# A relational graph sum on one core: its last 1024 nodes as dense products instead of gathered edge tiles

## The chip, the cores and the metric

The kernel runs on one core of a Trainium2 chip. The core has five engines that run side by side, each through its own list of instructions: PE (matrix products), DVE (vector), ACT (scalar functions), POOL (general, and the one that issues the gathers) and SP (which issues plain DMAs). They meet at semaphores only. The metric is the device time of one execution in microseconds (us), lower is better.

## The reference

There are N = 3125 nodes with D = 128 features and E = 103125 edges, sorted by destination. 3125 of them are loops; on average 33 edges end at a node.

```
# first part: 3 graph convolutions, a linear layer on all 4 states
h = elu(segment_sum((h @ W.T)[src] * dinv[src] * dinv[dst], dst) + b) + h     # 3 times
x = layernorm(x + concat(h0, h1, h2, h3) @ lin_w.T + lin_b)
# second part, the "second sum": 8 relations from 4 bases
W[r] = sum over b of w_comp[r, b] * bases[b]
msg  = x[src] * edge_weight
agg[r, n] = sum of msg over the edges of type r that end at n
x = layernorm(x + sum over r of agg[r] @ W[r])
```

All four bases can be summed first: for each node n and base b, A[b, n] = sum over its edges of (edge_weight * w_comp[type, b]) * x[src], and the result is the sum over b of A[b, n] @ bases[b]. Both kernels compute it so.

## The kernel before, in words

**Layers.** The 3 convolutions go as dense products: the adjacency is built on the chip as counts (one-hots by DVE at L865, products on PE at L1134, copied to bytes by ACT at L719, in blocks of 20 nodes), and PE multiplies with it in 7 column chunks of 480 nodes a layer (L1145). PE is busy nearly all of this time. Small DVE work between the chunks (the line numbers round L904, L923) computes `coef`, the edge's weight times the 4 base coefficients, for all 806 tiles. The linear layer (L1232) and the first layernorm follow; its result x1 is stored to memory by SP (L584).

**Second sum.** The edges are cut into 806 tiles of 128 (one edge per partition). 33 tiles make a chunk, meant for 128 destination nodes, and there are 25 chunks (the last has 14 tiles). Each tile takes three steps:

- POOL gathers the tile's 128 source rows of x1 from memory with one indirect DMA (`gathers`, L661), 11 tiles to a group. Ahead of a group it waits until DVE has written the group's indices (`indices`, L1002) and until PE is done with the group's old rows (a wait on `s_mu`, tile done, L654), and runs a tiny operation (L659).
- DVE makes a 128x192 matrix (`moving`, L1012): for each edge a one-hot of its destination in a window of 48 nodes, times its 4 coefficients. There are MS = 3 buffers, so DVE waits before tile j until PE has signalled that tile j - 3 is done.
- PE multiplies the gathered rows with it (`tile`, L1252), adding into PSUM banks 2, 0, 1 (nodes before, in and after the chunk); 12 of 33 tiles straddle two banks and need two products. A product of fp32 numbers appears as two passes in the trace. Every tile raises `s_mu`.

Once per chunk come the `fold` on DVE (L1020, L1021: banks 0 and 1 to SBUF), three products with zeros on PE that clear the banks (L1265), the sum `aggf` (L1050), 4 products with the bases (`finish`, L1258), and the layernorm (L1028 to L1038, root on ACT at L778), stored by SP. The previous chunk's closing work lies between the tiles of the next one. The engines' programs are written out by hand in this order, as loops over chunks.

Of the kernel before, what the change touches and what calls it, by code (L numbers as in the profile page):

```python
# [16 lines left out]
def build_program(nc, x, src, dst, etype, eweight, conv_w, conv_b, lin_w, lin_b, bases, w_comp, out):  # L17
# [18 lines left out]
    NCHK = -(-TILES // TPB)  # L36
    LTILES = TILES - TPB * (NCHK - 1)
    LNODES = N - P * (NCHK - 1)
# [33 lines left out]
    with ctx:  # L72
# [6 lines left out]

        arena = sb("arena", [P, ADJ], bf16)  # L80
# [60 lines left out]
        flagf = carve(47904, 4, fp32, 4)  # L141
        excess = sb("excess", [P, 1], fp32)
# [11 lines left out]
        srcI = carve(14592, TILES, u32, 4)  # L154
        dl = carve(17920, TILES, fp32, 4)
        wE = carve(RB + 12544, TILES, fp32, 4)
        tyE = carve(RB + 15872, TILES, fp32, 4)
        linbB = carve(RB + 19200, D, fp32, 4)
        coef = carve(2 * RB + 12800, TILES * NB, fp32, 4).rearrange("p (t b) -> p t b", b=NB)
        relw = carve(2 * RB + 25696, TILES, fp32, 4)  # L160
        xb = carve(4 * RB, NBLK * D, fp32, 4).rearrange("p (s d) -> p s d", s=NBLK)
        acc = carve(4 * RB + 12800, NB * P, fp32, 4)
        carry = carve(4 * RB + 14848, NB * P, fp32, 4)
        aggf = carve(4 * RB + 16896, NB * P, fp32, 4).rearrange("p (b n) -> p b n", b=NB)
        bnst = carve(4 * RB + 18944, UBT * 8, fp32, 4).rearrange("p (t s) -> p t s", t=UBT)
        mv = carve(4 * RB + 19072, NBLK * 2, fp32, 4).rearrange("p (t s) -> p t s", s=2)
        rstd = carve(4 * RB + 19328, NBLK, fp32, 4)
        iota_w = carve(4 * RB + 19456, WN, fp32, 4)
        shift = carve(4 * RB + 20224, NBLK, fp32, 4)
        iota_wf = carve(4 * RB + 19712, P, fp32, 4)  # L170
        ystage = carve(4 * RB + 20480, 2 * D, fp32, 4).rearrange("p (s d) -> p s d", s=2)
        fst = carve(4 * RB + 21504, 16, fp32, 4)
        idxg = carve(4 * RB + 21632, TPB, u32, 4)
        x1r = carve(2 * RB, NCHK * D, fp32, 4).rearrange("p (s d) -> p s d", s=NCHK)
# [33 lines left out]
        x1_d = nc.dram_tensor("x1_scratch", [N, D], fp32, kind="Internal").ap()  # L208

        ps = ctx.enter_context(nc.psum_tensor("ps", [P, 8, 512], fp32))  # L210


        s_dst = sem("dst_loaded")
        s_raw = [sem(f"edges_loaded{a}") for a in range(4)]
# [1088 lines left out]
```

## Time and profile before

| | |
|---|---|
| 3 runs | 1859.42, 1865.01 (median), 1873.81 us |
| profiled execution | 1863.87 us, of which its span is 1862.1 us (1.8 us lie around it) |
| busy share of the span | PE 62%, DVE 43%, POOL 44%, ACT 14% |
| busy time | PE 1147.9 us, DVE 792.9, POOL 820.8, ACT 257.6 |
| granted TensorE clock, mean | 0.698 of full |
| first gather of the second sum to the end | from 563.5 to 1862.1 us |

The profile page is one execution. It gives busy time by engine, the span in 40 slices, the groups of instructions that cost most with the idle time before them and what ended it, and the chain that ended last. The timeline rows give the start of an operation, its length, and in brackets how long its engine had been idle and whose signal ended that: "issue" is no signal at all that the profile shows, "remote" one that it cannot assign.

### The profile page before, as it was taken

Reading aid. Unit: us, or ns where it says so; the run is one execution under the profiler, and the core shown is the slowest. Engines: PE = TensorE matmul, PEld = TensorE weight load, DVE = VectorE, ACT = ScalarE, POOL = GpSimd, SP = SyncE. Lnnn points to the kernel's source line nnn. Section 1 sums busy time; section 2 is a strip of 40 time slices with the busy share of each in tenths; the row PEclk is TensorE's granted clock in tenths of the full one; section 3 lists DMA queues with packets and bytes.
Section 4 is the critical chain, followed back from the end, with each engine's and each line's share of the span. In section 5 each row is a group of like instructions: output and inputs, shape, how many; then the busy total and the mean of one; then the engine's idle time right before and its main releaser. Section 6 shows DMA issues by size and latency. Waiting matters only on the chain.

```text
span 1862.1 us, 18954 instructions
## 1 busy us (share of the span) xinstructions
PE 1147.9 (62%) x6042; PEld 841.1 (45%) x6042; DVE 792.9 (43%) x1636; ACT 257.6 (14%) x630; POOL 820.8 (44%) x931
## 2 busy tenths in 40 slices
PE   2478999999982455555554555565545455555446
PEld 2455666455471344344443434444434333444445
DVE  3798996455661333233332232333323323333324
ACT  3498894002030000000000000000000000000000
POOL 4220000000006666665555656655556556556562
PEclk8679999999995656556655655656565656656666
DMA  4500001001112111111111111111111111111110
GB/s 126 178 15 2 1 1 35 1 1 35 35 27 88 43 45 42 47 45 41 41 39 41 42 41 45 48 39 41 38 41 45 39 44 47 41 41 44 39 44 24
DMA packets 51315, 77.86 MB, mean 42 GB/s; under 512 B 18282, under 2 KB 35159, under 8 KB 50628
## 3 DMA queue, kind: packets, MB, share of 16 engines
q0 software_dynamic: 26512, 54.60, 10.6%
q1 hardware_dynamic: 24756, 22.61, 4.1%
q8 instruction: 32, 0.52, 0.1%
q14 instruction: 15, 0.12, 0.0%
HBM read 65.48 MB, written 6.88 MB: 39 GB/s over the span
## 4 chain that ended last, share of the span: by engine, by line
PE 43%; another core or an unknown queue 19%; DVE 16%; issue 14%; DVEq 3%; DMA 2%; POOL 1%; ACT 1%; SPq 0%; ACTq 0%; POOLq 0%
PE ps L1252 24%; PE ps L1145 13%; DVE arena L1012 6%; DVE arena L865 4%; DVEq L1012 2%; PE ps L1265 2%; PE ps L1258 2%; PE ps L1134 1%; PE ps L1232 1%; DVE arena L1021 1%; DVE arena L1020 1%; PE ps L1161 1%; DVE arena L847 1%; POOL arena L627 1%
## 5 line engine op out<-in xcount | busy, mean ns | idle before, releaser
L1252 PE MATMUL ps<-arena 128*128 128x192 f32 (+9 forms) x2200 | 616.9, 440 | 562.2 <-DVE arena L1012 413.0
L661 POOL DMA_INDIRECT arena<-x_scratch,arena x806 | 761.6, 945 | 241.0 <-issue 233.7
L1252 PEld LDWEIGHTS ps<-arena 128*128 128x128 f32 x2200 | 489.3, 291 | 694.2 <-DVE arena L1012 500.2
L1012 DVE SCALAR_TENSOR_TENSOR arena<-ps,arena 128x192 f32<-128x192 f32 x806 | 323.6, 416 | 877.4 <-remote 389.2
L1145 PE MATMUL ps<-arena,u 125*128 125x480 fp8e5 (+1 forms) x1575 | 359.7, 353 | 0.5 <-ACT arena L721 0.5
L1145 PEld LDWEIGHTS ps<-arena,u 125*128 125x128 bf16 x1575 | 151.0, 97 | 103.8 <-ACT arena L721 1.0
L865 DVE TENSOR_TENSOR arena<-arena 128x2048 bf16<-128x2048 bf16 (+2 forms) x158 | 188.7, 1254 | 11.0 <-PE ps L1134 7.2
L778 ACT ACTIVATE arena<-arena,epst 128x1 f32<-128x1 f32 x25 | 7.4, 294 | 1293.4 <-issue 891.9
L642 POOL IOTA arena<- 128x48 f32 x1 | 0.2, 176 | 396.0 <-PE ps L1145 396.0
L1134 PE MATMUL ps<-arena 128*128 128x125 bf16 x1256 | 149.0, 233 | 33.8 <-DVE arena L865 31.8
L1134 PEld LDWEIGHTS ps<-arena 128*128 128x128 bf16 x1256 | 107.0, 104 | 85.4 <-DVE arena L865 49.6
L659 POOL TENSOR_TENSOR arena<-epst 128x1 f32<-128x1 f32 x74 | 14.5, 195 | 293.4 <-issue 178.5
L721 ACT ACTIVATE arena<-ps,minus 128x500 bf16<-128x500 f32 x157 | 109.7, 699 | 0.0
L719 ACT CAST arena<-ps 128x500 fp8e5<-128x500 f32 x157 | 91.4, 582 | 37.2 <-PE ps L1134 36.0
L1265 PE MATMUL ps<-arena 128*128 128x512 bf16 x75 | 36.5, 625 | 57.7 <-DVE arena L1021 51.3
L904 DVE TENSOR_TENSOR work<-ps,dinv_all 128x480 f32<-128x480 f32 (+1 forms) x21 | 13.0, 621 | 101.7 <-PE ps L1145 101.7
L923 DVE SCALAR_TENSOR_TENSOR arena<-arena,compB 128x806 f32<-128x806 f32 x28 | 47.0, 1680 | 1.0
L1258 PEld LDWEIGHTS ps<-arena 128*128 128x128 f32 x200 | 45.9, 318 | 2.3 <-DVE arena L1065 2.3
L1258 PE MATMUL ps<-arena 128*128 128x128 f32 x200 | 45.3, 403 | 2.0 <-DVE arena L1065 2.0
L736 ACT ACTIVATE work<-work 128x480 f32<-128x480 f32 (+1 forms) x21 | 12.2, 579 | 197.4 <-DVE work L906 197.4
L1265 PEld LDWEIGHTS ps<-arena 128*128 128x128 bf16 x75 | 7.0, 123 | 70.3 <-DVE arena L1021 56.8
L721 ACT ACTIVATION_READ_ACCUMULATOR arena<-ps,minus 128x1 f32 x157 | 34.4, 219 | 0.0
(124 smaller groups left out, 507.2 us busy)
## 6 DMA issues: line engine op xcount, KB each, us to landing
arena<-x_scratch,arena POOLq DMA_INDIRECT x806
arena<-hT SPq DMA_DIRECT2D x3, 1562.5 KB, 7.1
arena<-in_x_dram SPq DMA_DIRECT2D x2, 1562.5 KB
edge_scratch<-arena SPq DMA_DIRECT2D x5, 403.0 KB, 6.1
arena<-edge_scratch SPq DMA_DIRECT2D x4, 403.0 KB, 15.2
dinv_all<-dinv_scratch SPq DMA_DIRECT2D x1, 1562.5 KB, 13.8
h_scratch<-hT SPq DMA_DIRECT2D x1, 1562.5 KB, 11.0
out_dram<-arena SPq DMA_DIRECT2D x24, 64.0 KB
```

Of the source, the lines that this page charges most:

```text
L627: nc.gpsimd.indirect_dma_start(out=win[:, b, 0:WUSE], out_offset=None, in_=edges_of[a], in_offset=bass.IndirectOffsetOnAxis(ap=idx_w[:, b: ...
L661: nc.gpsimd.indirect_dma_start(out=gat[:, j, :], out_offset=None, in_=x1_d, in_offset=bass.IndirectOffsetOnAxis(ap=idxg[:, j:j + 1], axis= ...
L719: nc.scalar.copy(region[:, :, at:at + GN], ps[:, 3 + k % SLOTS, 0:GN * NBLK].rearrange("p (n s) -> p s n", s=NBLK), saturate=False).then_i ...
L721: nc.scalar.activation(above[k % SLOTS], counts, ACT.Relu, bias=minus7[:, 0:1], accum_out=over[:, k:k + 1]).then_inc(s_adj, 1)
L865: V.tensor_tensor(hot[pair][a][:, 0:GRP * groups, 0:w, :], iota_v[:, None, 0:w, :].broadcast_to([P, GRP * groups, w, 2]), codes[:, :, None ...
L923: link(V.scalar_tensor_tensor(coef[:, :, b], relw[:, :], s, coef[:, :, b], ALU.mult, ALU.add))
L1012: V.scalar_tensor_tensor(mov[:, j % MS, :, :], ps[:, 4:5, 0:WN].broadcast_to([P, NB, WN]), dl[:, ds(c * TPB + j, 1)], coef[:, ds(c * TPB + ...
L1134: last = T.matmul(ps[:, 3 + slot, QW * g:QW * (g + 1)], hot[slot // 2][0][:, GRP * (slot % 2) + g, :, h], hot[slot // 2][1][:, GRP * (slot ...
L1145: return T.matmul(ps[:, agg_bank(l, c), 0:CW[c]], u[0:BLK, s, k, :], region[:, s, 0:CW[c]], start=(first and s == 0 and k == 0), stop=(end ...
L1252: last = T.matmul(o, gat[:, j, :], mov[:, j % MS, :, a - LO[j]:b - LO[j]], start=False, stop=False, skip_group_check=True)
L1258: last = T.matmul(ps[:, 3, 0:D], aggf[:, b, :], basesS[:, b, :], start=(b == 0), stop=(b == NB - 1))
L1265: T.matmul(ps[:, bank, 0:NB * P], zeros[:, 0:P], zeros[:, 0:NB * P], start=True, stop=False, skip_group_check=True)
```

## The change

The gathered tiles now serve only the first SN = 2101 nodes: 17 chunks with 548 tiles (the last chunk has 53 nodes and 20 tiles). The last 1024 nodes are 16 half-chunks of 64 nodes, one beside each full chunk. For each half-chunk h:

- **Quads (built in chunk h).** A node has a window of 64 consecutive edges from its first one; two nodes share the 128 partitions. For an edge from source s = 125 v + w, ACT makes a one-hot of w (125 wide; `onehots`, 4 Abs and one Relu for 4 columns, that is 8 nodes) and DVE a one-hot of v times the 4 coefficients (100 wide; `quad`, 4 operations). PE multiplies them, 8 products of 64 rows for 8 nodes (`quad`), into banks 6 and 7, and ACT copies both banks (125x400 each) into `sD` (`evict`). This makes a dense matrix of 3125 sources by 64 nodes by 4 bases. Eight quads a chunk, after tiles 3, 7, ..., 31. Banks 6 and 7 are single: PE waits for the copy of the quad before.
- **Dense products (in chunk h + 1).** 25 products 125x128 by 125x256 of x1, which lies in SBUF, with `sD`, one after each of the tiles 4 to 28 (`dense`), into bank 5; then ACT copies them, and PE multiplies with the bases (`finish_dense`), with a layernorm of its own.

Around it, tiles go in batches of BT = 3: one `s_mu`, one `s_m` and one gather semaphore for three tiles, with MS = 4 batches of moving buffers (12 tiles) in place of 3 tiles. POOL's groups are 12, 12 and 9 tiles and no longer wait on `s_mu` themselves; the indices on which they wait come after DVE's own wait. The windows are prepared in the layers: 5 small DVE operations and a store and 8 loads of node starts, 32 indirect gathers of 64 edges per partition on POOL, 3 conversions, 16 transposes on PE (ahead of the second layer's products with the adjacency) with 4 copies on ACT, 8 DVE operations 512 wide; `coef` has 1062 columns in place of 806. A graph in which a node's edges do not fit is sent down the general branch by the same flag as before.

```diff
-    NCHK = -(-TILES // TPB)
+    BT = 3
+    TB = TPB // BT
+    GB = [0, 12, 24, TPB]
+    DN = 64
+    DH = 16
+    SN = N - DN * DH
+    NCHK = -(-SN // P)
+    LTILES = -(-(LNODES * TPB) // P) + 6
+    TS = TPB * (NCHK - 1) + LTILES
+    QD = 8
...
-        MS = 3
+        MS = 4
...
+            flat = [a.rearrange("(n o) -> n o", o=1) for a in (dst, src, etype, eweight)]
+            for a in range(4):
+                for g in range(PG):
+                    for w in range(2):
+                        nc.gpsimd.indirect_dma_start(out=rawD[a][:, g, DN * w:DN * w + DN], out_offset=None, in_=flat[a],
...
                 def gathers(c, first, count=TPB):
-                    for g in range(-(-count // GG)):
+                    for g in range(sum(1 for a in GB if a < count)):
                         pool.wait_ge(s_idx, 3 * c + g + 1)
-                        if not first:
-                            pool.wait_ge(s_mu, TPB * c - TPB + GG * (g + 1))
...
+                def onehots(c, k):
+                    for i in range(4):
+                        ins = nc.scalar.activation(hotD[:, k % 2, i, :], iota_l[:, :], ACT.Abs, bias=nloD[:, ds(c * (4 * QD) + (4 * k + i), 1)])
...
+                    nc.scalar.activation(hq, hq, ACT.Relu, bias=onesf[:, 0:1], scale=-1.0).then_inc(s_ho, 1)
+                def evict(c, k, half):
+                    act.wait_ge(s_sb, c * QD + (k + 1))
+                    for w in range(2):
+                        at = DN // 2 * w + 4 * k
+                        ins = nc.scalar.copy(sD[half][0:BLK, :, at:at + 4], ps[0:BLK, 6 + w, 0:4 * NB * NBLK].rearrange("p (n m) -> p m n", n=4))
...
+                def moving(c, q, head, n=BT):
+                    if q >= MS:
+                        dve.wait_ge(s_mu, c * TB + (q - MS + 1))
+                    elif not head and q < TB % MS:
+                        dve.wait_ge(s_mu, c * TB - (TB % MS - 1 - q))
+                    for i in range(n):
...
+                        if i == n - 1:
+                            ins.then_inc(s_m, 1)
+                def quad(c, k, head):
+                    if not head or k >= 2:
+                        dve.wait_ge(s_sb, c * QD + (k - 1))
...
                 def tile(c, j, count):
-                    if j % GG == 0:
-                        pe.wait_ge(s_g[j // GG], c * (16 * GG) + 16 * min(GG, count - j))
-                    pe.wait_ge(s_m, c * TPB + (j + 1))
+                    q = j // BT
+                    if j % BT == 0:
+                        pe.wait_ge(s_g[q], c * (16 * BT) + 16 * min(BT, count - j))
+                        pe.wait_ge(s_m, c * TB + (q + 1))
...
-                    last.then_inc(s_mu, 1)
+                    if j % BT == BT - 1 or j == count - 1:
+                        last.then_inc(s_mu, 1)
+                def quad(c, k, head):
+                    pe.wait_ge(s_ho, c * QD + (k + 1))
+                    pe.wait_ge(s_md, c * QD + (k + 1))
+                    if not head or k >= 1:
+                        pe.wait_ge(s_se, c * QD + k)
+                    for i in range(4):
+                        for w in range(2):
+                            last = T.matmul(ps[0:BLK, 6 + w, NB * NBLK * i:NB * NBLK * (i + 1)], hotD[DN * w:DN * w + DN, k % 2, i, :],
+                                            movD[DN * w:DN * w + DN, k % 2, i, :, :].rearrange("p b v -> p (b v)"), start=True, stop=True)
+                    last.then_inc(s_sb, 1)
+                def dense(s, half):
+                    last = T.matmul(ps[:, 5, 0:NB * DN].rearrange("p (b n) -> p b n", b=NB), xb[0:BLK, s, :],
+                                    sD[half][0:BLK].rearrange("p (b v) n -> p b v n", b=NB)[:, :, s, :], start=(s == 0), stop=(s == NBLK - 1))
...
+                        if rank >= 1:
+                            if j == 4:
+                                pe.wait_ge(s_se, c * QD)
+                            for s in ((j - 4,) if count == TPB else (2 * j - 8, 2 * j - 7)):
+                                if 0 <= s < NBLK:
+                                    dense(s, 1 - half)
+                        if count == TPB and j % 4 == 3 and j // 4 < QD:
+                            quad(c, j // 4, rank == 0)
+                        if j == 14 and rank >= 1:
+                            finish(c - 1, rank)
```

PE's list at the start of a chunk of the second sum, before: the zero products (L1265), then tiles (L1252), each with a wait of its own on DVE (moving_ready).

```order
L1265 MATMUL ps<-arena 128x512 [waits chunk_folded]
L1265 MATMUL ps<-arena 128x512 x2
L1244 ISA
L1245 ISA [waits gathered0]
L1252 MATMUL ps<-arena 128x4x21 [waits moving_ready]
L1252 MATMUL ps<-arena 128x4x27
L1245 REGISTER_ALU
L1252 MATMUL ps<-arena 128x4x18 [waits moving_ready]
L1252 MATMUL ps<-arena 128x4x30
```

The same place in the changed kernel, from the second batch on (L1494 is the tile, L1506 the quad, L1512 the dense product):

```order
L1487 REGISTER_ALU [waits gathered1]
L1494 MATMUL ps<-hT,arena 128x4x10 [waits moving_ready]
L1494 MATMUL ps<-hT,arena 128x4x38
L1500 ISA
L1506 MATMUL ps<-hT,dinv_all 125x100 [waits quad_copied,dense_moving_ready,source_onehots_ready]
L1506 MATMUL ps<-hT,dinv_all 125x100 x7
L1494 MATMUL ps<-hT,arena 128x4x6
L1494 MATMUL ps<-hT,arena 128x4x42
L1512 MATMUL ps<-arena 128x256 [waits quad_copied]
L1494 MATMUL ps<-hT,arena 128x4x2
L1494 MATMUL ps<-hT,arena 128x4x46
L1512 MATMUL ps<-arena 128x256
```

A tile waits once for three now; between the tiles stand the quads, which wait on ACT's copy of the quad before, and the dense products, which wait for nothing after the first.

DVE's list at the start of a chunk, before (L1012 moving, L1020 and L1021 the fold):

```order
L1012 ISA [waits tile_done]
L1012 REGISTER_ALU
L1012 SCALAR_TENSOR_TENSOR arena<-ps,arena 128x192
L1011 REGISTER_ALU
L1012 ISA [waits tile_done]
L1012 ISA
L1012 SCALAR_TENSOR_TENSOR arena<-ps,arena 128x192
L1019 ISA
L1020 TENSOR_TENSOR arena<-ps,arena 128x512 [waits tile_done]
```

The same place in the changed kernel (L1199 moving, L1187 the indices of POOL's next group, L1211 quad):

```order
L1187 COPY arena<-arena 128x12
L1197 REGISTER_ALU
L1199 ISA [waits tiles_done]
L1199 SCALAR_TENSOR_TENSOR hT<-ps,arena 128x192
L1199 ISA
L1199 SCALAR_TENSOR_TENSOR hT<-ps,arena 128x192
L1199 ISA
L1199 SCALAR_TENSOR_TENSOR hT<-ps,arena 128x192
L1209 ISA
L1211 ISA [waits quad_built]
L1211 REGISTER_ALU
L1211 SCALAR_TENSOR_TENSOR hT<-ps,arena 128x100
```

One wait on PE now covers three tiles, and there is a second kind of wait on PE, for quads. The indices of the second and third group of gathers come behind these waits.

## Rows read from the trace of the kernel before

**Rows 1.** Busy us of each engine in two stretches; then clock, DMA share, GB/s.

```profile
230.00:529.00 299.00, 292.40 (x2030) 170.89 (x2029) 187.29 (x221) 82.95 (x192) 1.16 (x3) 1.00 0.06 17
640.00:1832.00 1192.00, 638.82 (x2297) 501.33 (x2297) 377.21 (x1026) 6.77 (x23) 722.99 (x820) 0.60 0.15 43
```

**Rows 2.** The page's groups: count, busy us, mean ns, idle before and releaser.

```profile
L1252 PE MATMUL ps<-arena 128*128 128x192 f32 (+9 forms) x2200 | 616.9, 440 | 562.2 <-DVE arena L1012 413.0
L661 POOL DMA_INDIRECT arena<-x_scratch,arena x806 | 761.6, 945 | 241.0 <-issue 233.7
L1012 DVE SCALAR_TENSOR_TENSOR arena<-ps,arena 128x192 f32<-128x192 f32 x806 | 323.6, 416 | 877.4 <-remote 389.2
```

**Rows 3.** Timeline (start us, length us, engine): a fold, POOL's next group starts, and the 12th fold on.

```profile
1218.52 0.69 DVE L1020 TENSOR_TENSOR arena<-ps,arena 128x512 f32<-128x512 f32 x1 [0.23 <-PE ps L1252]
1218.62 0.19 POOL L659 TENSOR_TENSOR arena<-epst 128x1 f32<-128x1 f32 x1 [9.33 <-issue]
...
1235.15 0.19 POOL L659 TENSOR_TENSOR arena<-epst 128x1 f32<-128x1 f32 x1 [2.44 <-PE ps L1252]
...
1840.19 0.69 DVE L1020 TENSOR_TENSOR arena<-ps,arena 128x512 f32<-128x512 f32 x1 [0.46 <-PE ps L1252]
```

**Rows 4.** Timeline of DVE in the stretch before that fold, POOL gathering until 1209.29.

```profile
1204.13 0.42 DVE L1012 SCALAR_TENSOR_TENSOR arena<-ps,arena 128x192 f32<-128x192 f32 x1 [3.82 <-remote]
...
1209.73 0.42 DVE L1012 SCALAR_TENSOR_TENSOR arena<-ps,arena 128x192 f32<-128x192 f32 x1 [5.18 <-issue]
...
1213.23 1.07 DVE L1012 SCALAR_TENSOR_TENSOR arena<-ps,arena 128x192 f32<-128x192 f32 x3 [3.01 <-remote]
```

**Rows 5.** Timeline of DVE in the first chunk, while POOL gathers three groups without a pause.

```profile
607.74 0.42 DVE L1012 SCALAR_TENSOR_TENSOR arena<-ps,arena 128x192 f32<-128x192 f32 x1 [4.48 <-remote]
609.14 1.07 DVE L1012 SCALAR_TENSOR_TENSOR arena<-ps,arena 128x192 f32<-128x192 f32 x3 [0.99 <-remote]
```

**Rows 6.** Timeline of the head: POOL's ten gathers, and ACT copying PE's transposes.

```profile
26.88 1.68 POOL L627 DMA_INDIRECT arena<-in_dst_dram,idx_w  x1 [8.90 <-DVE idx_w L824]
...
39.34 0.94 POOL L627 DMA_INDIRECT arena<-in_src_dram,idx_w  x1 [0.30 <-issue]
```

**Rows 7.** Timeline of ACT and of PE in the same stretch.

```profile
37.76 1.11 ACT L683 COPY hT<-ps 128x500 f32<-128x500 f32 x2 [0.26 <-PE ps L1090]
40.35 0.57 ACT L683 COPY hT<-ps 128x500 f32<-128x500 f32 x1 [1.48 <-PE ps L1090]
41.75 0.74 ACT L683 COPY hT<-ps 128x500 f32<-128x500 f32 x2 [0.82 <-remote]
...
34.96 4.25 PE L1090 MATMUL ps<-ident,arena 125*128 125x125 f32 x25 [8.83 <-DMA arena<-in_x_dram]
```

**Rows 8.** Timeline of PE: passes at full clock (first row) and at half clock.

```profile
544.89 0.82 PE L1232 MATMUL ps<-linT,arena 128*125 128x128 f32 x6
...
1219.99 1.46 PE L1265 MATMUL ps<-arena 128*128 128x512 bf16 x3 [1.51 <-DVE arena L1021]
1221.24 7.03 PE L1252 MATMUL ps<-arena 128*128 128x84 f32 x28
1237.05 1.91 PE L1258 MATMUL ps<-arena 128*128 128x128 f32 x8
```

**Rows 9.** The group of the 125x128 activations on ACT.

```profile
L769 ACT ACTIVATE arena<-arena 125x128 f32<-125x128 f32 x25 | 10.2, 481 | 0.6
```

**Rows 10.** Timeline of ACT in the first layer: the first and fifth of five blocks.

```profile
108.99 0.57 ACT L719 CAST arena<-ps 128x500 fp8e5<-128x500 f32 x1 [0.87 <-PE ps L1134]
...
113.72 0.59 ACT L719 CAST arena<-ps 128x500 fp8e5<-128x500 f32 x1
```

**Rows 11.** Timeline: the second sum's first gather, PE's first tiles, and the last store.

```profile
563.54 0.96 POOL L661 DMA_INDIRECT arena<-x_scratch,arena  x1 [0.45 <-issue]
...
578.62 6.79 PE L1252 MATMUL ps<-arena 128*128 128x84 f32 x26 [19.64 <-DMA arena<-x_scratch,arena]
...
1858.88 0.26 SPq L598 DMA_DIRECT2D out_dram<-arena  x1
```

More of the change, by code:

```diff
@@ L560, in _ @@
             sp.dma_start(dinv_all[:, :], dinv_d[0:N].rearrange("(o n) -> o n", o=1).broadcast_to([P, N])).then_inc(s_dinva, 16)
+            sp.wait_ge(s_std_d, 16)
+            starts = start_d[SN:N].rearrange("(g h w p) -> h w p g", g=PG, h=4, w=2)
+            with nc.allow_non_contiguous_dma(reason="a word per node"):
+                for h in range(4):
+                    for w in range(2):
+                        sp.dma_start(wposf[32 * h:32 * h + 32, PG * w:PG * w + PG], starts[h, w]).then_inc(s_stl, 16)
             sp.wait_ge(s_ev, NJ)
@@ new lines, in chunk @@
+                def chunk(c, rank, half, following=True):
+                    for k in range(QD):
+                        if k == 0 and rank >= 2:
+                            act.wait_ge(s_dp, c - 1)
+                        evict(c, k, half)
+                        if k < QD - 2:
+                            onehots(c, k + 2)
+                        elif following:
+                            onehots(c + 1, k + 2 - QD)
+                        if k == 0 and rank >= 2:
+                            root_dense(c - 2)
+                        if k == 4 and rank >= 1:
+                            root(c - 1)
+                        if k == 6 and rank >= 1:
+                            copy_dense(c - 1)
@@ new lines, in _ @@
+                onehots(0, 0)
+                onehots(0, 1)
+                chunk(0, 0, 0)
+                chunk(1, 1, 1)
+                with act.Fori(1, DH // 2 - 1) as i:
+                    chunk(i * 2, 2, 0)
+                    chunk(i * 2 + 1, 2, 1)
+                chunk(DH - 2, 2, 0)
+                chunk(DH - 1, 2, 1, following=False)
+                root_dense(DH - 2)
+                root(NCHK - 2)
+                copy_dense(DH - 1)
+                root_dense(DH - 1)
+                root(NCHK - 1)
@@ L1020, in fold @@
+                def fold(c, batches=TB):
+                    dve.wait_ge(s_mu, c * TB + batches)
                     link(V.tensor_tensor(acc[:, :], ps[:, 0, 0:NB * P], carry[:, :], ALU.add))
@@ L1200, in _ @@
             for l in range(1, LAYERS):
+                if l > 1:
+                    pe.wait_ge(s_rel, l - 1)
                 for j in range(NUB):
@@ L1205, in _ @@
                     products(l, j)
+                if l == 1:
+                    pe.wait_ge(s_wflt, 3)
+                    for a in range(4):
+                        for g in range(PG):
+                            last = T.transpose(ps[:, 1 + a, P * g:P * (g + 1)], rawDf[a][:, g, :], ident[:, :])
+                        last.then_inc(s_wjob, 1)
                 for c in range(NCH):
+                    if l == 1 and c == 1:
+                        pe.wait_ge(s_wev, 4)
                     if c >= 5:
@@ L1259, in finish, with finish_dense, chunk @@
                     last.then_inc(s_fin, 1)
-                def chunk(c, head, count=TPB):
-                    if not head:
+                def finish_dense(h):
+                    pe.wait_ge(s_da, h + 1)
+                    pe.wait_ge(s_fv, h + 1)
+                    for b in range(NB):
+                        last = T.matmul(ps[0:DN, 3, 0:D], aggD[:, b, :], basesS[:, b, :], start=(b == 0), stop=(b == NB - 1))
+                    last.then_inc(s_df, 1)
+                def chunk(c, rank, half, count=TPB):
+                    if rank >= 1:
                         pe.wait_ge(s_fold, c)
```

343 lines of the change are left out of this document (249 added, 94 removed).

## The prediction

> **What bounds the kernel now.** I read the stretches first. In the layers, 230 to 529 us, PE is busy 292.4 of 299 us at full clock; in the second sum, 640 to 1832 us, no engine is: PE 638.8 of 1192 us at a mean clock of 0.60, POOL 723.0, DVE 377.2 [rows 1]. So the 1292 us that the change works on are a matter of waits. The groups say which: PE waits on DVE's moving matrices, and DVE waits 877 us before them, 389 of these on something the profile cannot assign [rows 2]. The gathers have a rate of their own, (761.6 + 241.0) / 806 = 1.244 us each [rows 2]: 33 of them and three small operations of 0.19 us are a floor of 41.6 us a chunk. The timeline has twelve chunks between two folds, (1840.19 - 1218.52)/12 = 51.8 us each [rows 3].
>
> The timeline then shows why it isn't 41.6. POOL pauses 9.33 and 2.44 us before two of the groups of a chunk [rows 3], and the pauses come from PE's signals being late. Near 1204 us DVE makes a tile's matrix only every 4.2 to 5.6 us, its idle time before one being 3.82 and 5.18 us, although a tile costs PE about 1 us at half clock; each waits for the tile three before, so a signal arrives some 12.6 us after its tile. POOL stops gathering at 1209.3, and at 1213.2 three DVE operations run back to back: the held signals arrive together [rows 4]. In the first chunk, where POOL gathers without a pause, the step is 4.90 us until 607.7, and then again three at once [rows 5]. The same happens far from here with other work: in the head POOL issues ten gathers from 26.88 to 40.28 us; PE's transposes run through in 4.25 us from 34.96, ACT copies the first four promptly, and the last three start at 40.35 and 41.75, when POOL has stopped [rows 6, 7]. **My reading: once POOL has gathered for about 9.5 us without a pause (26.9 to 38 us there, 11 us; a chunk's first slow tile is 9 to 10 us after POOL resumes), PE's completion signals come one per 2 to 5.6 us, until POOL pauses for 1.5 to 4 us.** What in the chip does this no row shows; DVE's signals to PE and POOL are not late.
>
> **The change part by part.**
>
> *Stage start.* The second sum's first gather is at 563.5 us [rows 11]. Added ahead of it: 16 fp32 transposes on PE, which is saturated there: 16 x 4.25/25 = 2.7 us [rows 7]; five small chained DVE operations in the head, about 0.3 us each, 1.5 us; the 32 window gathers, 40 us on POOL, beside the building of the adjacency. There PE hands a block to ACT every (113.72 - 108.99)/4 = 1.18 us [rows 10], with four PSUM slots. By my reading signals are late for 40 - 9.5 = 30 us of it: at 2.1 us a block, 14 blocks instead of 26, a loss of 13 us; at 4.9, a loss of 23; if late signals spare them, 0. I take 12. The 28 wider coefficient operations and the 8 window operations lie on DVE beside PE's products (DVE 187 of 299 us busy [rows 1]); cover gone, they would cost some 20 us, which I leave to the range. Start: 563.5 + 16.2 = 580 us.
>
> *A full chunk, PE.* Tiles: 90 passes (33 tiles, 12 of them doubled), at half clock 7.03/28 = 0.251 us each, 22.6 us [rows 8]. Quads, new: 64 products, 128 passes of 100 columns with 125-column weights. Nearest is the pass of 128 columns: eight take 1.91 us at half clock [rows 8], of which the last one's tail overlaps, and the starts are 0.213 us apart; six take 0.82 us at full clock, starts 0.109 apart. So 27.3 or 14.0 us. Dense, new: 25 products of 256 columns, 50 passes at twice that: 21.3 or 10.7. Finishes, 16 passes: 3.4 or 1.7. Zeros: 1.46 or 0.7, and 1.5 us in which PE waits for the fold [rows 8]. Sum: 77.5 us a chunk at half clock, 40 at full. The quads' 64-row products have no row in this trace; below by half (two at a time), above by nothing that I see.
>
> The Trainium skill (TensorE: Matmul & The Clock Gate, Part 3: Packing small matmuls) says that products on different row groups run concurrently in the array; the quads' pairs, on partitions 0 to 63 and 64 to 127, are such. By it the quads would take 7 us a chunk at full clock in place of 14. No row here shows it; it is a rival below.
>
> *POOL*: unchanged per tile, 41.6 us a chunk, but for 548 tiles in place of 806: 258 x 1.244 = 321 us of floor gone. *DVE*: 33 operations of 0.42 us, 32 smaller ones at about 0.25, folds, sums and two layernorms, about 27 us. *ACT*: 32 Abs at 0.41 to 0.48 [rows 9], 8 Relus and 16 copies at about 0.6: 29 us. Neither bounds.
>
> *Waits.* Twelve tiles of look-ahead in place of three: a signal that is 12.6 us late no longer stops DVE. But a quad's signal goes PE to ACT, and ACT's to PE, with one buffer, and behind it in PE's list stand the tiles. A chunk now has 11 + 8 + 3 = 22 completion signals of PE. At 4.2 us each, slow stretches proceed at 92 us per chunk (46 at 2.1; 123 at 5.6). POOL gathers 41.6 us per chunk; with T above that it pauses about twice (its third group waits for the fold, its first for batch 4), and each pause gives 9.5 us free: 41.6 - 19 = 22 us slow, in which 22/92 = 0.24 of a chunk is done. The rest at full clock takes 0.76 x 40 = 30 us. **T = 22 + 30, taken as 53 us.** I take 4.2 because it is the step that half of the slow stretches in mid-chunk show; no lateness at all would give POOL's 41.6 and small gaps, T = 44.
>
> *Ends.* First chunk: PE starts after three gathers, 5 us, not after eleven (15.1 us [rows 11]); the last chunk has 20 tiles and 25 dense products, about 22 us; closing, 5 us before and a second layernorm, 8 us; around the span 1.8.
>
> **Sum: 580 + 16 x 53 + 5 + 22 + 8 + 1.8 = 1465 us**, against 1863.87 of the profiled execution, 1.1 us under the median, so no correction. A chunk more or less of 1 us is 16 us in the total; break-even is T = (1865 - 617)/16 = 78 us.
>
> **The rivals.**
> 1. *Signals are not late for batches and quads* (they belong to the register wait on three small buffers). For: the head's four prompt copies. Against: the head's three late ones, which are plain handshakes [rows 7]. POOL bounds, T = 44: 580 + 704 + 37 = 1321. Chance 0.20.
> 2. *The quads' halves run side by side*: T = 22 + 0.76 x 33 = 47 to 48: 1377. Chance 0.08.
> 3. *The clock is mixed*, as in the second sum now (0.60 [rows 1]): 60 us per chunk fast, T = 22 + 46 = 68: 1705. Chance 0.17.
> 4. **Slower: PE stays at half clock.** Each quad makes PE stop for ACT's copy, in fast stretches too; if these stops hold it at 1.2 GHz, as the stops for DVE do near 1204 us, T = 22 + 0.76 x 77.5 = 81: 580 + 1296 + 37 = 1913. It decides from T = 78 on, that is if less than a tenth of the work runs at full clock. For: most of the second sum is at half clock now. Against: there PE sits idle half the time, and with three times the passes it will not; in the layers, busy at 98%, it is at full clock throughout [rows 1]. Chance 0.11.
> 5. *It does not do what it says*: if a node had more than 64 edges, or a tile's window missed, the flag would send all engines down the general branch, far slower. The drawn graph's largest node has 58. 0.02. The same time as before by chance: 0.02.
>
> The Trainium skill (TensorE: Matmul & The Clock Gate, A second HAM failure mode: psum-queue depth-cycling) says that PE swings between its clock levels where short idles come with each turn of the PSUM banks. This would speak for rivals 3 and 4, since banks 6 and 7 turn eight times a chunk; before, the mean of 0.60 agrees with such swinging.
>
> **How the numbers follow.** The forecast's own case (T from 48.5 to 60: 1390 to 1580) has 0.40. Below it lie rivals 1 and 2, above it 3 and 4. Range 1310 to 1750: it takes in rivals 1, 2 and most of 3, with the head's 0 to 23 us, and leaves out 4 and 5, the tail of 3 and a little below. A measurement of this kernel tells about 1% from no change. Faster by over 1% (below 1846): 0.40 + 0.20 + 0.08 + 0.17 = 0.85; within 1%: 0.02; slower: 0.13.
>
> **What the profile of the changed kernel would show.** Folds 53 us apart in the full chunks (44 with rival 1, 68 or 81 with 3 or 4). L1506 eight times a chunk, each first pass behind an idle of several us ended by ACT's evict where POOL has gathered over 9.5 us, and hardly any where it has paused. PE's clock above 0.75 in the second sum. POOL pauses of 5 us or more before two of its three groups; if the gathers stand back to back, rival 1 holds. The first gather at 580 us; at 568 if the window gathers delayed nothing in the layers. L1506 passes starting in pairs would be rival 2. I am wrong at the root if quads wait for DVE (L1211) or for ACT's one-hots rather than for the copies, or if POOL's idle time stems from the indices standing behind DVE's quad waits: then the tiles, not the signals, were starved.

## The result, and the profile after

The changed kernel took 1697.33 us (median of 4, 1689.16 to 1709.3) against 1865.78: ratio 0.910, 95% interval 0.903 to 0.917. It is faster, by 168 us where 400 were forecast. The profiled execution took 1700.38 us (span 1698.5). The comparisons of this study fell into two kinds, in which the same kernel before took either 1854 to 1882 us ("slowing", this result among them) or 1595 to 1600 us ("plain"), and times below are compared within their kind.

The page's clock slices and the stretch of the full chunks of the changed kernel (busy us of each engine, then clock, DMA share, GB/s), which answer to [rows 1]:

```profile
PEclk8666899999999956868867768878668688577588
640.00:1640.00 1000.00, 710.76 (x4380) 605.33 (x4381) 364.70 (x1271) 350.46 (x911) 482.19 (x547) 0.75 0.13 34
```

The page's groups, which answer to [rows 2]:

```profile
L742 POOL DMA_INDIRECT arena<-x_scratch,arena x548 | 517.8, 945 | 159.3 <-issue 153.0
L1494 PE MATMUL ps<-hT,arena 128*128 128x192 f32 (+8 forms) x1492 | 375.4, 376 | 51.6 <-issue 37.3
L879 ACT COPY arena<-ps 125x400 f32<-125x400 f32 x256 | 113.5, 495 | 705.0 <-remote 420.4
L1211 DVE SCALAR_TENSOR_TENSOR hT<-ps,arena 128x100 f32<-128x100 f32 x512 | 128.8, 314 | 334.5 <-remote 202.2
L740 POOL TENSOR_TENSOR arena<-epst 128x1 f32<-128x1 f32 x50 | 9.7, 194 | 420.2 <-DVE arena L1187 372.9
```

A gather costs what it did, 1.24 us. POOL is not the bound: it stands idle 420 us before its groups, 373 of them for indices, and these stand behind DVE's waits on PE. This is one of the signs by which the prediction said it would be wrong; it does not name the cause, since the same order of work is there in the plain runs below, where POOL hardly waits. ACT's copies of the quads and DVE's quad operations wait on PE's completions, mostly marked "remote". Folds 0 and 15 are at 685.7 and 1663.7 us, so a full chunk takes 65.2 us.

The timeline around one fold, which answers to [rows 3] and [rows 4]:

```profile
1140.22 0.69 DVE L1221 TENSOR_TENSOR arena<-ps,arena 128x512 f32<-128x512 f32 x1 [11.85 <-remote]
1141.70 1.46 PE L1536 MATMUL ps<-arena 128*128 128x512 bf16 x3 [11.17 <-DVE arena L1222]
1142.04 0.19 POOL L740 TENSOR_TENSOR arena<-epst 128x1 f32<-128x1 f32 x1 [4.14 <-DVE arena L1187]
...
1168.01 0.19 POOL L740 TENSOR_TENSOR arena<-epst 128x1 f32<-128x1 f32 x1 [14.69 <-DVE arena L1187]
...
1182.09 0.94 POOL L742 DMA_INDIRECT arena<-x_scratch,arena  x1 [0.30 <-issue]
1185.45 0.89 ACT L879 COPY arena<-ps 125x400 f32<-125x400 f32 x2 [12.08 <-remote]
1185.60 1.01 DVE L1211 SCALAR_TENSOR_TENSOR hT<-ps,arena 128x100 f32<-128x100 f32 x4 [10.21 <-remote]
```

POOL gathers from 1168.3 to 1183.0 us. The quad that stands in PE's rows from 1173.3 to 1174.4 is reported at 1185.4, 2.4 us after POOL has stopped. Meanwhile ACT, DVE and PE stand. PE's own rows in that gap show that it is more than a late report:

```profile
1175.97 0.49 PE L1494 MATMUL ps<-hT,arena 128*128 128x192 f32 x2
1176.30 0.38 PE L1512 MATMUL ps<-arena 125*128 125x256 f32 x1
1177.58 0.38 PE L1512 MATMUL ps<-arena 125*128 125x256 f32 x1 [0.90 <-issue]
1178.29 0.56 PE L1494 MATMUL ps<-hT,arena 128*128 128x180 f32 x2 [0.34 <-issue]
1179.71 0.17 PE L1494 MATMUL ps<-hT,arena 128*128 128x12 f32 x1 [0.85 <-issue]
1180.42 0.28 PE L1494 MATMUL ps<-hT,arena 128*128 128x12 f32 x1 [0.54 <-issue]
```

These passes wait for no semaphore ("issue") and still stand 0.7 to 1.4 us apart; before 1176.3 the rows stand at full rate. In the layers, under the window gathers (117 to 162 us), ACT's block copies, 1.1 us apart up to 129.9, thin out; they answer to [rows 10]:

```profile
149.43 0.57 ACT L800 CAST arena<-ps 128x500 fp8e5<-128x500 f32 x1 [4.46 <-PE ps L1366]
159.95 0.57 ACT L800 CAST arena<-ps 128x500 fp8e5<-128x500 f32 x1 [9.28 <-remote]
165.63 0.57 ACT L800 CAST arena<-ps 128x500 fp8e5<-128x500 f32 x1 [4.43 <-PE ps L1366]
```

In a plain run of the same kernel (c1_after below) they stay about 1.1 us apart there, and from 145 to 166 us PE is busy 16.7 us against 7.0 here. The second sum's first gather comes at 597.1 us.

The clock is at its lower level after each stop of PE: it was 0.50 from 1140 to 1152 us and 1.00 from 1156 to 1176. The same 16 passes of a quad take 2.00 us in the one and 1.12 in the other:

```profile
1146.61 2.00 PE L1506 MATMUL ps<-hT,dinv_all 64*125 64x100 f32 x16
1155.26 1.12 PE L1506 MATMUL ps<-hT,dinv_all 64*125 64x100 f32 x16
```

### The profile page after: what moved, and what is told of

Its sections match the earlier page's. It is cut to its first block, busy times and chain, and to the rows that moved or that the text cites. A ratio compares the mean times of both kernels' runs of the same rounds, so it can differ in the third digit from the quotient of the medians.

```text
span 1698.5 us, 23701 instructions
## 1 busy us (share of the span) xinstructions
PE 1236.0 (73%) x8238; PEld 957.6 (56%) x8238; DVE 776.7 (46%) x1908; ACT 616.4 (36%) x1554; POOL 610.1 (36%) x686
## 4 chain that ended last, share of the span: by engine, by line
PE 51%; another core or an unknown queue 21%; DVE 10%; issue 8%; ACT 4%; DMA 3%; POOL 1%; DVEq 1%; ACTq 0%; POOLq 0%
PE ps L1377 14%; PE ps L1494 13%; PE ps L1512 9%; PE ps L1506 8%; DVE arena L1023 5%; PE ps L1366 2%; PE ps L1536 1%; PE ps L1475 1%; DVE hT L1211 1%; ACT dinv_all L865 1%; PE ps L1522 1%; DVE hT L1199 1%; PE ps L1393 1%; DMA dinv_col<-dinv_scratch 1%
## 5 line engine op out<-in xcount | busy, mean ns | idle before, releaser
L742 POOL DMA_INDIRECT arena<-x_scratch,arena x548 | 517.8, 945 | 159.3 <-issue 153.0
L1494 PE MATMUL ps<-hT,arena 128*128 128x192 f32 (+8 forms) x1492 | 375.4, 376 | 51.6 <-issue 37.3
L1494 PEld LDWEIGHTS ps<-hT,arena 128*128 128x128 f32 x1492 | 307.0, 253 | 102.9 <-issue 56.8
L1512 PE MATMUL ps<-arena 125*128 125x256 f32 x800 | 272.0, 423 | 19.2 <-issue 19.1
L1211 DVE SCALAR_TENSOR_TENSOR hT<-ps,arena 128x100 f32<-128x100 f32 x512 | 128.8, 314 | 334.5 <-remote 202.2
L1506 PE MATMUL ps<-hT,dinv_all 64*125 64x100 f32 x2048 | 183.8, 320 | 130.6 <-ACT arena L879 61.3
L1506 PEld LDWEIGHTS ps<-hT,dinv_all 64*125 64x125 f32 x2048 | 157.2, 223 | 173.9 <-issue 163.9
L1199 DVE SCALAR_TENSOR_TENSOR hT<-ps,arena 128x192 f32<-128x192 f32 x548 | 191.4, 410 | 79.6 <-PE ps L1494 59.3
L1512 PEld LDWEIGHTS ps<-arena 125*128 125x128 f32 x800 | 158.3, 213 | 23.8 <-issue 23.0
L865 ACT ACTIVATE dinv_all<-arena 128x125 f32<-128x125 f32 x512 | 162.6, 398 | 0.0
```

Source lines behind the costliest of these rows:

```text
L742: nc.gpsimd.indirect_dma_start(out=gat[:, j, :], out_offset=None, in_=x1_d, in_offset=bass.IndirectOffsetOnAxis(ap=idxg[:, j:j + 1], axis= ...
L865: ins = nc.scalar.activation(hotD[:, k % 2, i, :], iota_l[:, :], ACT.Abs, bias=nloD[:, ds(c * (4 * QD) + (4 * k + i), 1)])
L1199: ins = V.scalar_tensor_tensor(mov[:, q % MS, i, :, :], ps[:, 4:5, 0:WN].broadcast_to([P, NB, WN]), dl[:, ds(c * TPB + (BT * q + i), 1)], ...
L1211: ins = V.scalar_tensor_tensor(movD[:, k % 2, i, :, :], ps[:, 4:5, 0:NBLK].broadcast_to([P, NB, NBLK]), hiD[:, ds(c * (4 * QD) + (4 * k + ...
L1494: last = T.matmul(o, gat[:, j, :], mov[:, q % MS, j % BT, :, a - LO[j]:b - LO[j]], start=False, stop=False, skip_group_check=True)
L1506: last = T.matmul(ps[0:BLK, 6 + w, NB * NBLK * i:NB * NBLK * (i + 1)], hotD[DN * w:DN * w + DN, k % 2, i, :], movD[DN * w:DN * w + DN, k % ...
```

## The experiments

Two theories stood against each other at first: A, PE is slowed once POOL has gathered for some 9 us without a rest; B, the waits come from the order of the work on DVE and POOL. All kernels below differ from the changed one by the edit shown, except where the kernel before is named. "Chunk" is the mean distance of the folds of full chunks. The first result, c1_after, e5_serial and e15_headrest are medians of four executions, e1_rest, e4_headrest and e6_traffic of two; each other kernel ran once. e2_third and the nodense kernels leave work out, as said below, and their times serve the argument only.

| run | kind | us | chunk | kernel before beside it |
|---|---|---|---|---|
| the changed kernel, first result | slowing | 1697.3 | 65.2 | 1865.8 |
| c1_after, the changed kernel | plain | 1275.3 | 41.3 | 1596.6 |
| c2_before, the kernel before | plain | 1597.9 | 41.4 | 1596.6 |
| c3_after, the changed kernel | slowing | 1701.1 | 66.3 | 1860.2 |
| e1_rest, 5 rests of 1.3 us | plain | 1371.6 | 47.4 | 1595.7 |
| e2_third, a third of the gathers | plain | 1191.8 | 36.6 | 1595.7 |
| e3_nodense / e11_nodense | plain | 1274.8 / 1277.4 | 41.5 | 1595.7 / 1595.4 |
| e12_nodense | slowing | 1498.6 | 53.2 | 1882.2 |
| e4_headrest, 5 rests of 0.3 us and rests in the layers | plain | 1291.7 | 42.3 | 1595.7 |
| e5_serial, quads' halves one after the other | plain | 1276.3 | 41.2 | 1597.0 |
| e6_traffic | plain | 1282.5 | 41.7 | 1597.0 |
| e8_longrest, 5 rests of 2.6 us and rests in the layers | slowing | 1489.4 | 54.2 | 1860.2 |
| e7_beforerest, the kernel before with 5 rests of 2.6 us | slowing | 1901.2 | 53.9 | 1860.2 |
| e9_midrest / e13_midrest, 5 rests of 1.3 us and rests in the layers | plain / slowing | 1369.5 / 1614.5 | 47.4 / 60.8 | 1595.4 / 1882.2 |
| e10_threerests / e14_threerests, 3 rests of 2.6 us and rests in the layers | plain / slowing | 1399.6 / 1541.6 | 49.0 / 57.7 | 1595.4 / 1882.2 |
| e15_headrest, rests in the layers only | slowing | 1687.9 | 65.4 | 1859.8 |

**First comparison: rests, fewer gathers, no dense part.** The rest in `gathers` (e4_headrest has 64 columns in place of 512):

```diff
+                PAUSES = [3, 10, 16, 23, 29]
...
+                            if j in PAUSES:
...
+                                nc.gpsimd.tensor_tensor(work[0:BLK, 0, 0:512], work[0:BLK, 1, 0:512], work[0:BLK, 2, 0:512], ALU.add).then_inc(s_rest, 1)
                             nc.gpsimd.indirect_dma_start(out=gat[:, j, :], out_offset=None, in_=x1_d,
```

> The changed kernel with a rest for POOL (one addition of 125x512 numbers, 1 to 2 us, in place of the next gather) before tiles 3, 10, 16, 23 and 29 of each chunk, so that POOL never gathers more than 7 tiles in a row. Theory A (PE is slowed only after POOL has gathered for some 9 us without a rest): the slow stretches vanish, folds about 52 to 55 us apart instead of 65, total about 1500 to 1540. Rival B (the wait comes from the order of DVE's and POOL's work, not from POOL's gathering): POOL only gets more to do, folds stay at 65 us or rise by up to 8, total 1697 to 1820.

e2_third gathers one tile in three, `for j in range(GB[g], min(count, GB[g + 1]), BT)`, and PE multiplies its rows three times:

> The changed kernel with one gather for each batch of three tiles (the products read its rows three times; two thirds of the gathers are left out). POOL then gathers 4, 4 and 3 in a row. Theory A: no slow stretch in the second sum; a chunk is PE's own work with the quads' halves side by side, 33 to 40 us, total about 1200 to 1290. Rival B: the quads' handshakes and the fold keep a chunk at 55 us or more, total above 1500.

e3_nodense drops the calls of `onehots`, `evict`, `quad`, `dense`, `finish_dense` and their waits:

> The changed kernel without its dense part: no one-hots, no quads, no dense products and no dense finish (the last 1024 nodes get no result), all gathers left. Theory A: PE is still slow after 9 us of gathering, but 12 tiles of look-ahead hide half of it: folds 45 to 50 us apart. Rival C (PE's signals hurt only handshakes with quads): POOL's floor, 42 to 44 us.

e4_headrest also has three `iota` after every sixth window gather:

> The changed kernel with rests for POOL among the 32 window gathers of the layers (three index fills of about 0.65 us after every sixth gather), and in the second sum rests at the same five tiles as in the other run, but only 0.3 to 0.5 us long. Theory A in the layers: the first gather of the second sum comes at 565 to 575 us instead of 597. Rival B: it stays at 597 or later. In the second sum this shows how long a rest must be: with 0.4 us, if a short rest is enough, folds 45 to 55 us apart; if it must be 1.5 us or more, 65.

The comparison turned out to be plain: the kernel before took 1595.7 us. So it says nothing of the slowing; the rests here only add their length (47.4 = 41.4 + 5 x 1.2), and I could not yet tell A from B. It does give the other bounds: without the dense part the chunk is 41.5 us, POOL's floor, and with a third of the gathers 36.6 us, PE's own pace with quads, dense products and fold (PE is busy 519.9 of the 530 us from 620 to 1150).

**Second comparison: both kernels as they are.**

> The changed kernel as it is, beside the kernel before on this chip, where the kernel before took 1596 us in the last comparison and not 1865. Theory A (PE is slowed by POOL's long gathering, on this chip less than on the first one): folds 42 to 50 us apart, total 1290 to 1400, a ratio near 0.85. If PE is slowed here as in the first trace: folds 65 us apart, total 1697.

> The kernel before with a profile, on this chip. At 1596 us its chunks must be about 42 us, POOL's floor of 41.6 for 33 gathers, in place of 53. Theory A: the tile steps of 4.2 us on DVE are gone, and folds stand 41 to 43 us apart. Rival: the steps remain and something else (layers, head) is faster by 270 us.

Plain again. The changed kernel took 1275.34 us against 1596.56, ratio 0.799 (0.798 to 0.800). Folds of c1_after, then of c2_before:

```profile
908.16 0.69 DVE L1221 TENSOR_TENSOR arena<-ps,arena 128x512 f32<-128x512 f32 x1 [0.52 <-PE ps L1494]
949.68 0.69 DVE L1221 TENSOR_TENSOR arena<-ps,arena 128x512 f32<-128x512 f32 x1 [0.63 <-PE ps L1494]
```

```profile
907.39 0.68 DVE L1020 TENSOR_TENSOR arena<-ps,arena 128x512 f32<-128x512 f32 x1
948.58 0.68 DVE L1020 TENSOR_TENSOR arena<-ps,arena 128x512 f32<-128x512 f32 x1
```

Both stand at POOL's floor, 41.5 and 41.2 us apart. The gain, 321 us, is the 258 gathers that are gone at 1.244 us each (321 us); the whole dense part hides beside the remaining ones. That the two agree to the microsecond is luck in part: the first gather comes 6 us later than before (572.5 against 566.9), and the rest of the stage is shorter by about as much. In c1_after PE is busy 568 of 620 us at full clock (the stretch from 620 to 1240 us):

```profile
620.00:1240.00 620.00, 568.40 (x4303) 471.10 (x4303) 356.97 (x1236) 338.74 (x881) 475.62 (x539) 0.99 0.20 55
```

**Third: the quads' halves, and other traffic.**

```diff
-                    for i in range(4):
-                        for w in range(2):
+                    for w in range(2):
+                        for i in range(4):
```

> The changed kernel with the quads' products in another order: the four on partitions 0 to 63 first, then the four on 64 to 127, where the changed kernel alternates. If the alternating pairs run side by side (starts 0.01 us apart in the trace of the changed kernel), a quad becomes nearly twice as long, 16 passes in about 1.8 to 2.0 us instead of 1.12, and PE's chunk goes from 36.5 to about 42 or 43 us: folds 42 to 44 us apart instead of 41.4, total 1280 to 1320. If the order does not matter: 1.12 us and 1275.

A quad in the timeline of c1_after, then of e5_serial:

```profile
902.82 1.12 PE L1506 MATMUL ps<-hT,dinv_all 64*125 64x100 f32 x16
```

```profile
903.76 1.63 PE L1506 MATMUL ps<-hT,dinv_all 64*125 64x100 f32 x16
```

So the alternating products do run side by side: 1.12 us for 16 passes against 1.63. Single starts show it too: in c1_after two passes start 0.01 us apart and the next two 0.10 us on; in e5_serial one pass follows the other by 0.11 us, except in the middle of the quad, where some of the second half overlap the first. The total did not move (1276.3), since 8 x 0.5 = 4 us more a chunk still fit under POOL's 41.4. I had expected a chunk of 42 to 44.

e6_traffic adds `sp.dma_start(trash_d[:, :], h_d[0])` to SP's loop, 1.6 MB from memory to memory per chunk:

> The changed kernel with a copy of 1.6 MB within memory on SP's queue in each chunk, beside the gathers, so that the DMA engines and the memory move about three times as much. If other traffic is what slows PE behind POOL's gathers on the first chip, slow stretches appear here and folds go to 50 us or more, total above 1400. If the slowing has nothing to do with traffic: PE's signals stay prompt and the total is 1275 to 1290.

95 GB/s instead of 55, and 1282.5 us: traffic alone does not bring the slowing about in a plain comparison.

**Fourth: rests of 2.6 us, and this time the comparison was slowing.** Two additions instead of one at the same five tiles, in e8_longrest with rests in the layers too:

> The changed kernel once more, as a control for the chip of this comparison. Theory A says that a chip either slows PE behind long gathering or not: either 1275 us with the kernel before at 1597, or near 1697 with the kernel before near 1865. Rival D (the slowing depends on the hour or on the profile and not on the chip): something in between.

> The changed kernel with rests for POOL of 2.6 us (two additions of 125x512) before tiles 3, 10, 16, 23 and 29, and rests of some 2 us among the window gathers. On a chip that does not slow PE: POOL's floor plus 5 x 2.4, folds about 53 us apart, total about 1465. On one that does: theory A says the same 53 to 55 us, which there is a gain of 10 us a chunk and of 25 us in the layers (first gather near 570), total 1470 to 1520 against 1697.

> The kernel before with the same rests of 2.6 us at tiles 3, 10, 16, 23 and 29. On a chip that does not slow PE: chunks of about 53 us instead of 41.4, total about 1880. On one that does: theory A says no slow stretch, about 53 us as well, so the total stays near 1865 although POOL has 290 us more to do; the rival (rests only add) says 1865 + 290 = 2150.

This settles A against B, though not the 9 us in A. POOL is given about 13 us more to do in each chunk, and the changed kernel falls from 1701 to 1489 us; its chunk of 54.2 us is POOL's 41.4 plus the rests, the value that had been forecast; from 640 to 1440 us POOL is never idle for more than 0.5 us. The kernel before rises only from 1860 to 1901, where a mere addition would have given 2150: the rests take the place of most of the slowing. POOL is busy in a rest too, so it is the gathering that slows PE, not a busy POOL. One rest of e8_longrest and the next gather:

```profile
1002.94 2.63 POOL L757 TENSOR_TENSOR work<-work 125x512 f32<-125x512 f32 x2
1005.72 0.96 POOL L758 DMA_INDIRECT arena<-x_scratch,arena  x1
```

The slowing is not wholly gone with them. A mark of it is a pass that waits for no semaphore and yet starts over 0.5 us after PE went idle. From 560 us on, the traces of the changed kernel in slowing comparisons have 64 and 81 of these (first result, c3_after), e15_headrest 61, e12_nodense 49, e14_threerests 43, e13_midrest 26 and e8_longrest 15, one of them here; every plain run has none. In e8_longrest they cost nothing that shows, since POOL bounds.

```profile
1015.69 0.59 PE L1510 MATMUL ps<-hT,arena 128*128 128x100 f32 x4 [1.07 <-issue]
```

**Fifth and sixth: how long a rest, and the tiles' share.** The first of these comparisons was plain, the second slowing.

> Rests of one addition (1.28 us) before tiles 3, 10, 16, 23 and 29, and rests in the layers. On a chip that does not slow PE: 47 us a chunk as in the first run with rests, total about 1370. On one that does: if 1.3 us is enough to undo the slowing, 48 us a chunk and 1385; if a rest must be near 2.6 us, still 55 us or more, 1500 and above.

> Rests of 2.6 us before tiles 5, 16 and 27 only, so 11 gathers (13.7 us) in a row. On a chip that does not slow PE: 41.4 + 3 x 2.5 = 49 us, total about 1400. On one that does: about 4 us of slowing are left in each of three series; 50 to 54 us a chunk, total 1420 to 1490; without any effect of rests 65 or more.

> The changed kernel without its dense part (the last 1024 nodes get no result), all gathers left; on a chip that does not slow PE it took 41.4 us a chunk and 1275 us. On one that does: theory A with my formula (tiles only, 12 tiles of look-ahead, 12 signals a chunk) says 42 to 48 us a chunk; the kernel before, with 3 tiles of look-ahead, took 53.

> The changed kernel without its dense part (the last 1024 nodes get no result), all gathers left. On a chip that does not slow PE: 41.4 us a chunk, 1275 us. On one that does: 42 to 48 us a chunk by my formula (12 signals a chunk and 12 tiles of look-ahead), 53 or more if look-ahead does not help.

> Rests of 1.28 us at five tiles. On a chip that does not slow PE: 47 us a chunk, 1370. On one that does: 48 us and about 1385 if 1.3 us is enough, 55 us and 1500 or more if a rest must be near 2.6 us.

> Rests of 2.6 us at three tiles. On a chip that does not slow PE: 49 us a chunk, 1400. On one that does: 50 to 54 us a chunk, 1420 to 1490; without effect 65 or more.

Against plain, the slowing costs 13.4 us a chunk with rests of 1.3 us (60.8 against 47.4), 8.7 with three rests of 2.6 (57.7 against 49.0, a little above what I had expected), and nothing visible with five of 2.6, for which POOL's floor is the measure, since no plain run was made. Unrested it costs 24 to 25. Five rests of 1.3 us are not enough. But the kernels also differ in how long POOL rests in all, 6.4, 7.8 and 13 us a chunk, and the cost falls in that order; whether the length of a rest or the sum counts, no run separates.

e12_nodense is the one that hits my theory. Tiles alone, with 12 tiles of look-ahead, took 53.2 us a chunk, about the kernel before's with its 3 tiles [rows 3]; I had said 42 to 48. PE in it, around a series in which POOL gathers without a rest from 1022 to 1063 us, after a pause of 12.4 us:

```profile
1020.48 7.74 PE L1469 MATMUL ps<-hT,arena 128*128 128x192 f32 x48
1046.85 1.06 PE L1509 MATMUL ps<-arena 128*128 128x512 bf16 x2 [18.63 <-issue]
1047.71 5.31 PE L1469 MATMUL ps<-hT,arena 128*128 128x84 f32 x31
1055.49 0.32 PE L1469 MATMUL ps<-hT,arena 128*128 128x192 f32 x1 [2.47 <-issue]
1057.60 0.48 PE L1469 MATMUL ps<-hT,arena 128*128 128x192 f32 x1 [1.78 <-issue]
1059.70 0.48 PE L1469 MATMUL ps<-hT,arena 128*128 128x192 f32 x1 [1.62 <-issue]
```

Just after the pause 48 passes go in 7.74 us. Deep in the series single passes stand 2.1 us apart and wait for no semaphore; two make a tile, so this is the step of 4.2 us of [rows 4]. The 31 passes in 5.31 us between the two look prompt, right behind 18.6 us in which PE took in nothing. I take it that a row shows when PE takes a pass in, that some 30 fit, and that it then shows PE's true pace; this is an inference from the order of these rows. What is slow is then PE's rate, not the report of its work, and look-ahead does not help against a rate.

DVE's rows in the same trace say so independently. Its next two waits are for the signals of tiles 27 to 29 and of tiles 30 to 32:

```profile
1032.38 1.07 DVE L1182 SCALAR_TENSOR_TENSOR hT<-ps,arena 128x192 f32<-128x192 f32 x3 [5.43 <-remote]
1044.98 0.69 DVE L1204 TENSOR_TENSOR arena<-ps,arena 128x512 f32<-128x512 f32 x1 [11.54 <-remote]
```

They are 12.6 us apart, three times the step of the kernel before, which signals every tile; in all chunks between 760 and 1365 us it is 10.4 to 16.1 us, and 3.2 to 3.6 in e11_nodense. So the price goes by the work behind a signal and not by signals. It does not go by passes either: tiles 30 to 32 straddle two banks and have four passes each, and still take about 4.2 us a tile like the whole ones of two.

**Seventh: the layers alone.**

> The changed kernel with rests of about 2 us after every sixth of the 32 window gathers in the layers, and none in the second sum. On a chip that does not slow PE: first gather at 570 to 573 us as without them, total 1270 to 1276. On one that does: first gather at 575 to 582 us instead of 594, chunks 65 us as before, total about 1680 against 1701.

Slowing. The first gather came at 572.1 us instead of 594 to 597, as early as in plain comparisons (572.5); the chunk stayed at 65 us. With the same rests in the layers it came at 578.3 in e8_longrest, 582.2 in e13_midrest and 577.7 in e14_threerests, and at 604.2 in e12_nodense without them. The median is 1687.9 us, ratio 0.908 (0.905 to 0.912).

## Why the prediction was wrong

Total: 1700.4 - 1465 = 235 us in the profiled execution. By terms:

1. **The full chunk: 65.2 us where 53 stood. This is the step that failed**, "a signal that is 12.6 us late no longer stops DVE", and with it the count of 22 signals as what slow stretches process. It makes 15 x 12.2 = 183 us. The 22 signals at 4.2 us each were the wrong account: in e12_nodense one signal for three tiles takes 10.4 to 16.1 us, because what is slow is the work behind it. The passes themselves go at one in 0.7 to 2.8 us; I read the evenly spaced tiles as signals on their way, since PE's rows looked prompt. They would look so with never more than three tiles in its queue: the kernel before has none of the late passes that mark the slowing, in either kind. The tiles alone are 53.2 us in this state (e12_nodense), and with the change a chunk has three times the passes: 12 to 13 us on top, in which ACT, DVE and POOL wait for a quad. That share is the difference of two runs of different comparisons, not measured by itself. A second step failed beside it, "the rest at full clock takes 0.76 x 40 = 30 us": the clock is 0.50 after each stop, and PE is busy 46 us a chunk against 38 in c1_after (710.8 of 1000 us and 568.4 of 620), some 8 of the 24 us that the slowing costs.
2. **The start of the stage: 597 where 580 stood, 17 us.** The mechanism was the forecast one, the window gathers slow PE's blocks; its size was 25 us (597.1 - 572.1, e15_headrest), by the pairs within a comparison 16 (c3_after and e8_longrest) and 22 to 27 (e12_nodense against e13_midrest and e14_threerests), where I took 12 between ends of 0 and 23.
3. **First chunk and end: about 36 us.** The first fold came 89 us after the first gather where about 58 were implied; POOL gathers there from 596.4 to 638 us without any rest. The remaining 5 us lie behind the last full chunk.
4. Right: POOL's 1.244 us per gather, that the waits come with long gathering (the rests show that it is POOL's pauses which undo them), and that neither DVE nor ACT bounds. The onset after 9 us is right in kind only: it is 8 us here (1168.3 to 1176.3), but some 15 in the layers (first window gather at 117.0, copies late from about 132), and with rests of 1.3 us the slowing comes although no series is longer than 9 us. The clock was 0.75 in the full chunks; unslowed it is 0.99, so it follows from PE's stops, and then adds the share above. PE's chunk at full clock was put at 40 us and is 36.6 (e2_third), since the quads take 1.12 us each and not 1.75.
5. The rivals. The first (1321 us, POOL bounds with T = 44) is what plain comparisons give, 1275 and 41.3. I had it as a matter of how buffers work; it turned on which kind of comparison one is in, which one trace cannot tell. The second was right in its mechanism: 1.12 against 1.63 us a quad. Here the Trainium skill (TensorE: Matmul & The Clock Gate, Part 3: Packing small matmuls) holds: products on different row groups overlap, by a factor of 1.5 in these runs. It had no price, since PE did not bound in the plain state; in the slowing one it was not tried. The third gave nearly the measured total, 1705: a mixed clock is there, but it makes a third of the loss, and the agreement is luck. The fourth, PE at half clock throughout, did not come.

What stays open is what in the chip slows PE behind long gathering, why only some comparisons show it, and what it counts, if not signals or passes: columns, tiles or bytes. Other memory traffic of 40 GB/s does not bring it about in the plain state; in the slowing one neither that traffic nor fewer gathers (e2_third) was tried. The record numbers the chips: 12 and 5 were plain, 4 was slowing, 0 and 1 were each plain in one comparison and slowing in another. If a number is the same chip each time, which is not shown, the kind is not a fixed property of a chip.

The best version depends on the state. In the plain one the changed kernel as it is was the fastest full kernel, 1275 us. In the slowing one e8_longrest was, 1489 us against 1701 and 1860; its plain time was not run. By an estimate from e10_threerests, whose three rests a chunk cost 124 us over c1_after, it would be near 1480.

## What to carry to other kernels

If operations stand evenly spaced and wait on one engine, look in a stretch where that engine has a full queue: single passes that wait for nothing and are far apart point to a slow engine, and then look-ahead did not help here, while added work on that engine cost more than its plain time (12 to 13 us a chunk for the dense part, against none in the plain kind). Give POOL real pauses among its gathers (2.6 us after every 6 or 7 was enough, 1.3 us was not) where the trace shows such stretches, and not otherwise: in the plain kind the rests of 1.3 us cost 94 to 96 us. Take two comparisons before sizing a gain that hangs on a stretch no one can explain.

## What the runs showed of the hardware

- In four comparisons of eight, with POOL gathering without a rest, PE's fp32 passes of 192 columns fell from 0.16 us each (the 48 in 7.74 us, the first ones at half clock) to one in 2.1 to 2.8 us (e12_nodense); the onset was 8 us after the gathers began in the changed kernel. A rest of POOL of 2.6 us after 6 or 7 gathers brought the chunk from 66.3 to 54.2 us, though 15 late passes were left. It also hit the mixed bf16 and fp8 products in the layers, where PE was busy 7.0 of 21 us against 16.7.
- In that state three tiles with four passes each took 10.4 to 16.1 us (e12_nodense), about as much a tile as those with two passes: it is a price neither of a signal nor of a pass.
- The same kernel before took 1854 to 1882 us in some comparisons and 1595 to 1600 in others, and the changed kernel 1689 to 1709 or 1274 to 1277. The ratio was 0.91 in the one and 0.80 in the other.
- Two products of 64 rows on the two halves of the array overlap: 16 passes in 1.12 us alternating, in 1.63 us one half after the other.
